# A decoder layer on one core: the shared expert's gate and up in one PSUM bank each, and smaller edits around the router

## The chip, the core and the metric

The kernel runs on one core of one Trainium2 chip. The metric is the device time of one execution in microseconds (us). TensorE multiplies matrices into PSUM; VectorE (DVE), ScalarE (ACT) and GpSimd (POOL) work on SBUF, the first two on PSUM as well; SyncE (SP) issues most of the transfers. Each engine runs its own instructions in program order and waits for the others by semaphores.

## The reference: one pre-norm decoder layer with a mixture of experts

Input are 64 blocks of 128 tokens with 128 features, and a context of 77 rows for each block. In float32:

```
x = x + SelfAttn(layernorm(x))          # 16 heads of 8, rotary, causal
x = x + CrossAttn(layernorm(x), ctx)    # 16 heads of 8, 77 keys
n = layernorm(x)
probs = softmax(n @ router_w)           # 8 experts, the last one empty
e, p = argmax(probs), max(probs)        # one expert for each token
routed = down_e( up_e(n) * silu(gate_e(n)) )       # 0 where e is the eighth
shared = down_s( up_s(n) * silu(gate_s(n)) )       # hidden size 512
x = x + 2 * p * routed + shared
```

## The kernel before

The first stage is a software pipeline over the 64 blocks. On every engine, step i does pieces of several blocks: `at(i, p, lag, piece)` runs a piece for block i - lag, so one step holds one piece of each kind, of up to nine blocks. The order of the pieces inside a step is written out by hand for each engine, and it is this order that queues the work; no planner runs at build time. The first and the last steps are unrolled, the rest is a hardware loop over pairs of steps. The second stage sorts the tokens by expert (a routing table on VectorE, rows scattered to a buffer `xs` in HBM during the first stage) and runs 70 tiles of 128 tokens through their experts; the change doesn't touch its instructions.

PSUM has eight banks of 512 float32 columns. In the first stage:

- `scores` is four banks, used as two pairs. Pair 0 takes, in turn, half of the self-attention scores for the maximum (`self_max`), half of those for the exponential (`self_exp`), the same for the cross-attention, and the shared expert: gate in its first bank, up in its second.
- `pj` takes the projections of q, k, v and of the context, and two transposes.
- `st` takes float16 transposes: the stacked q and k (`stacks`, `stacks2`, L1232) and the row maxima (`nmT_of`, L1253).
- `pv` takes the attention output (`values`, L1122), 256 columns, which VectorE transposes out (`turned`, L647).
- `ro` takes output projections (`project_out`, L1131), transposes (`xT_of`, L1139), q of the cross-attention (L1150), the router, the token positions and the shared down projection (`shared_down`, L1177), each in its own columns.

A piece of TensorE that is about to overwrite a bank calls `turn(pe, b, *users)`: the first user that is in range gives the semaphore and the count for which it waits, which is the reader of the bank's last content.

The pieces around the change, in TensorE's order of one step, with the lines of the profile: `shared_gate` (L1163), `shared_up` (L1169), the cross output projection (L1131), `nmT_of` of the self-attention (the row maxima turned, L1253), `values` of the self-attention (L1122), `positions` (L1214, L1216, L1217), `cross_exp` and `cross_max` in two turns (L1033, L1025), the context transpose (L1223), `stacks` (L1232), `shared_down` (L1177). The next step goes on with the transpose of x (L1139), a second two-turn group, the self output projection (L1131), the context projection (L1228), the transpose of x1 (L1139), and the self-attention scores (L999, L1007, L1016).

The shared expert's chain through the engines: gate on TensorE, tanh on ScalarE (L877), `half_of` on VectorE (L721), `add_cross` on VectorE (L667, the cross-attention's residual), `hidden_of` on VectorE (L727, which sets `sh_hid`), then `shared_down`, then `add_shared` on VectorE (L733). `add_attention` (L660) adds the self-attention's residual, after which TensorE transposes x1.

The router on VectorE: `logits_copy` (L682), `top_of` (L687), `marks_of` (L691: logits equal to the top, times a mark, by a scalar operand of one value per partition), `mark_top_of` (L696), `hot_of` (L700: mark equal to its maximum, again by such a scalar). GpSimd meanwhile adds the rotary products (`rope_add`, L449) and their bias (`rope_bias_in`, L453). `positions` starts with an identity matmul that puts the running counts `run_base` into PSUM (L1214) and adds this block's counts to them; `run_of` (L712) copies the new counts back, and `hot_pos_of` (L707) picks each token's row. `carry` (L604) copies one column on VectorE so that a wait has an instruction of its own to sit on, ahead of the layer norms' `bn_aggr` (L625) and of the third layer norm's `bn_stats` (L619).

Of the kernel before, what the change touches and what calls it, by code (L numbers as in the profile page):

```python
# [13 lines left out]
P = 128  # L14
# [7 lines left out]
LAG = 11  # L22
LATE = 56
# [3 lines left out]
def decoder_layer(nc, x, ctx_in, sWq, sbq, sWk, sbk, sWv, sbv, sWo, sbo,  # L27
# [16 lines left out]
    assert S == P and D == P and NB % 16 == 0 and LATE % 4 == 0 and NB >= LATE + 4 and LATE + 10 >= NB and F == 4 * P and NT % 8 == 6 and ALPHA == 2.0  # L44

    with ExitStack() as stack:
# [116 lines left out]
        run_base = sb("run_base", [P, E])  # L163
# [44 lines left out]
        st16 = st[:, :].bitcast(F16)  # L208
# [37 lines left out]
        marked = sem("marked"); mark_topped = sem("mark_topped"); hot_ready = sem("hot_ready")  # L246
# [46 lines left out]
        def run(eng, step):  # L293


            first = (LAG + 3) // 2
# [5 lines left out]
            for i in range(NB, NB + LAG):  # L302
                step(i, i % 2)
# [44 lines left out]
        def _(sync):  # L348
# [24 lines left out]
            def load_x(b, p):  # L373
                if not isinstance(b, int) or b >= 2:
                    wait(sync, rot_summed, b - 1)
                    sync.dma_start(x_in[:, p, :], x[b]).then_inc(x_in_s[p], 16)
# [6 lines left out]

# [3 lines left out]
            def rows_of_max(b, p, n):  # L387

                wait(sync, nmT_ready[n], b + 1)
                for j in range(4):  # L390
                    sync.dma_start((qkT, qkT2)[n][SLOT * j + 3 * HD:SLOT * j + 3 * HD + HG, p, 0:HG * P].rearrange("p (g q) -> p g q", g=HG),
                                   nmaxT[SLOT * j:SLOT * j + HG, n, p, :].unsqueeze(1).to_broadcast([HG, HG, P])
                                   ).then_inc(max_rows[n][p], 16)
# [13 lines left out]
            run(sync, step_and_weights)  # L407
# [19 lines left out]
        def _(pool):  # L427
# [4 lines left out]
            def ln_rstd_of(b, p, n):  # L432

                wait(pool, ln_mv[n], b + 1)
                if n == 2:
                    g.tensor_tensor(neg_mean[:, :], mv[:, 2, p, 0:1], neg_one[:, :], ALU.mult)
                g.tensor_tensor(varp[:, n:n + 1], mv[:, n, p, 1:2], eps[:, :], ALU.add).then_inc(ln_var[n], 1)
                wait(pool, ln_var[n], b + 1)
                g.tensor_tensor(rstd[:, n, p:p + 1], varp[:, n:n + 1], neg_half[:, :], ALU.pow).then_inc(ln_rstd[n], 1)  # L439

            def ln3_shift_of(b, p):

# [4 lines left out]

# [9 lines left out]

# [17 lines left out]
            def scaled(b, p, n):  # L475
                wait(pool, o_recip[n], b + 1)
                g.tensor_tensor(by_head(otok[:, n, :]), ptok[:, n, :].rearrange("p (h s) -> p h s", s=SLOT // 2)[:, :, 0:HD],  # L477
                                rsum[:, n, :].unsqueeze(2).to_broadcast([P, H, HD]), ALU.mult).then_inc(o_scaled[n], 1)

            def add_out_bias(b, p, n):  # L480

                if n == 0:
                    wait(pool, x_in_s[p], 8 * b + 16 - 8 * p)
                g.tensor_tensor(resid[:, b, :], (x_in, x1)[n][:, p, :], out_bias[:, n, :], ALU.add).then_inc(xb_ready[n], 1)  # L484
# [5 lines left out]
            def scatter(b, p):  # L490
                wait(pool, scatter_going, b)
                wait(pool, put_ready, b + 1)
                wait(pool, sh_added, b + 1)
                g.tensor_tensor(carried[:, 4:5], eps[:, :], eps[:, :], ALU.add).then_inc(scatter_going, 1)
# [896 lines left out]
```

## Time and profile before

| | before |
|---|---|
| time, median of 3 runs | 1065.71 us (1065.3 to 1066.14) |
| the profiled execution, first to last instruction | 1065.7 us |
| PE / PE weight load / DVE / ACT / POOL busy | 992.5 / 818.3 / 870.9 / 737.2 / 631.4 us |
| first stage, from first to last residual of the self-attention (L660) | 55.0 to 807.2 us, 64 blocks |
| second stage, from the first tile's gate matmul | 856.95 us on |
| granted TensorE clock, mean | 0.990 |

Matmuls are pipelined, so "PE busy" says that instructions follow each other, not that the array is at its peak. A line such as L1122 stands for all the instructions that it issued; a helper's line stands for every use. An arrow `[0.23 <-DVE arena L656]` behind a row is the idle time ahead of it and what ended it.

### The profile page before, as it was taken

How to read it: one execution, taken by the hardware profiler on the slowest of the kernel's cores; microseconds unless marked ns; L12 is line 12 of the kernel's file. 1: busy time of each engine (PE TensorE's matmuls, PEld its weight loads, DVE VectorE, ACT ScalarE, POOL GpSimd, SP SyncE). 2: the span in 40 equal slices, each digit the busy share in tenths (PEclk: the TensorE clock that was granted, in tenths of full speed). 3: DMA queues.
4: the chain of work that ended last, by engine and by line, in shares of the span. 5: the costliest groups of instructions: out<-in, count | busy, mean ns of one | idle time of the engine just before them, and what ended most of it. 6: DMA issues, size and time to landing. Idle time of an engine off the chain costs nothing.

```text
span 1065.7 us, 45022 instructions
## 1 busy us (share of the span) xinstructions
PE 992.5 (93%) x16200; PEld 818.3 (77%) x16201; DVE 870.9 (82%) x2853; ACT 737.2 (69%) x1557; POOL 631.4 (59%) x1488
## 2 busy tenths in 40 slices
PE   1579999999999999999999999999999999999995
PEld 1357777777777777777777777777777889999995
DVE  4367999999999999999999999999986457777774
ACT  0267878888888878888888888887875145555552
POOL 0346677777777677777777777767764124444443
PEclk9999999999999999999999999999999899999998
DMA  6222011000100010000100010000000122222220
GB/s 133 71 72 77 28 32 32 26 30 26 32 26 30 25 29 28 26 30 26 32 26 30 26 29 28 30 25 28 28 29 21 58 70 70 73 71 68 70 65 5
DMA packets 66648, 44.27 MB, mean 42 GB/s; under 512 B 24135, under 2 KB 61451, under 8 KB 66592
## 3 DMA queue, kind: packets, MB, share of 16 engines
q1 hardware_dynamic: 55424, 30.35, 10.5%
q0 software_dynamic: 5312, 12.18, 3.3%
q10 hardware_dynamic: 5856, 0.99, 0.7%
q8 instruction: 36, 0.59, 0.2%
q14 instruction: 20, 0.16, 0.0%
HBM read 23.96 MB, written 18.29 MB: 40 GB/s over the span
## 4 chain that ended last, share of the span: by engine, by line
PE 76%; DVE 10%; issue 4%; SPq 3%; DMA 2%; ACT 1%; POOL 1%; ACTq 1%; DVEq 0%; POOLq 0%
PE pv L1122 11%; PE scores L1302 6%; PE scores L1307 6%; PE ro L1318 6%; PE ro L1177 6%; PE scores L1163 5%; PE st L1232 5%; DVE arena L641 4%; PE scores L999 4%; PE scores L1169 4%; PE ro L1139 3%; PE pj L1145 3%; PE ro L1131 3%; PE ro L1150 2%; PE scores L1033 2%
## 5 line engine op out<-in xcount | busy, mean ns | idle before, releaser
L919 ACT ACTIVATE arena<-scores 128x1024 f32<-128x1024 f32 (+1 forms) x256 | 262.6, 1026 | 48.5 <-PE scores L1016 33.6
L641 DVE TENSOR_REDUCE arena<-scores 128x8 f16<-128x1024 f32 (+1 forms) x256 | 256.7, 1003 | 47.5 <-PE scores L1007 37.6
L859 ACT ACTIVATE arena<-st 128x128 f16<-128x128 f16 (+2 forms) x256 | 154.9, 605 | 7.9 <-PE st L1232 6.8
L859 ACT ACTIVATE arena<-arena 128x512 f16<-128x512 f32 (+2 forms) x192 | 92.9, 484 | 70.3 <-POOL arena L453 50.3
L1122 PE MATMUL pv<-arena 128*32 128x128 f32 (+1 forms) x4096 | 139.3, 277 | 0.0
L1122 PEld LDWEIGHTS pv<-arena 128*32 128x32 f32 (+1 forms) x4096 | 104.6, 110 | 17.1 <-issue 10.1
L439 POOL TENSOR_TENSOR arena<-arena,neg_half 128x1 f32<-128x1 f32 x192 | 106.5, 555 | 15.0
L449 POOL TENSOR_TENSOR arena<-arena 128x256 f32<-128x256 f32 x64 | 46.4, 725 | 78.9 <-DVE arena L633 78.9
L526 POOL DMA_INDIRECT out_dram<-x_tile x70 | 69.9, 998 | 38.5 <-POOL carried L525 26.1
L477 POOL TENSOR_TENSOR arena<-arena 128x128 f32<-128x128 f32 x128 | 51.7, 404 | 61.2 <-DVE arena L651 61.2
L1232 PE MATMUL st<-id,arena 128*128 128x128 f16 (+1 forms) x1024 | 74.0, 215 | 8.5 <-POOL arena L462 8.5
L814 DVE SCALAR_TENSOR_TENSOR half_hid<-tanh_s,scores 128x512 f32<-128x512 f32 x70 | 48.1, 688 | 40.3 <-ACT tanh_s L964 40.2
L495 POOL DMA_INDIRECT xs<-pay,put x64 | 69.5, 1085 | 13.0 <-issue 13.0
L1302 PE MATMUL scores<-xT_tile,gate_tile 128*128 128x128 f32 x560 | 75.1, 278 | 1.9 <-ACT gate_tile L859 1.6
L1318 PE MATMUL ro<-w_down,hidT 128*128 x560 | 74.1, 275 | 0.9 <-DVE x_tile L826 0.9
L1307 PE MATMUL scores<-xT_tile,up_tile 128*128 128x128 f32 x560 | 74.5, 276 | 0.0
L1163 PE MATMUL scores<-arena,ws_gate 128*128 128x128 f32 x512 | 74.3, 288 | 0.0
L1177 PE MATMUL ro<-ws_down,hidT 128*128 128x128 f32 x512 | 71.2, 282 | 2.1 <-DVE hot_pos L707 1.9
L1232 PEld LDWEIGHTS st<-id,arena 128*128 128x128 f16 (+1 forms) x1024 | 63.4, 101 | 12.0 <-POOL arena L462 10.4
L484 POOL TENSOR_TENSOR resid<-arena,out_bias 128x128 f32 (+1 forms) x128 | 58.2, 454 | 23.4 <-DVE out_bias L600 23.4
L1302 PEld LDWEIGHTS scores<-xT_tile,gate_tile 128*128 128x128 f32 x560 | 69.0, 194 | 2.3 <-issue 1.7
L1318 PEld LDWEIGHTS ro<-w_down,hidT 128*128 128x128 f32 x560 | 68.0, 192 | 1.1 <-issue 1.1
(175 smaller groups left out, 2681.3 us busy)
## 6 DMA issues: line engine op xcount, KB each, us to landing
x_tile<-xs SPq DMA_DIRECT2D x70, 129.0 KB, 2.0
arena<-arena SPq DMA_DIRECT2D x512, 4.0 KB
arena<-in_x_dram SPq DMA_DIRECT2D x64, 64.0 KB, 1.8
out_dram<-pay SPq DMA_DIRECT2D x64, 64.0 KB, 1.6
arena<-in_ctx_dram SPq DMA_DIRECT2D x64, 38.5 KB
w_gate<-in_L_ffn_gate_w_dram SPq DMA_DIRECT2D x7, 256.0 KB, 2.8
w_up<-in_L_ffn_up_w_dram SPq DMA_DIRECT2D x7, 256.0 KB, 3.1
w_down<-in_L_ffn_down_w_dram SPq DMA_DIRECT2D x7, 256.0 KB, 4.0
```

Source lines behind the costliest of these rows:

```text
L439: g.tensor_tensor(rstd[:, n, p:p + 1], varp[:, n:n + 1], neg_half[:, :], ALU.pow).then_inc(ln_rstd[n], 1)
L526: g.indirect_dma_start(out=out_rows, out_offset=bass.IndirectOffsetOnAxis(ap=x_token[:, q, :], axis=0), in_=x_tile[:, q, D:2 * D], in_offs ...
L641: v.tensor_reduce(nmax[:, n, :].rearrange("p (m r s) -> p r m s", r=2, s=SLOT)[:, u, :, 0:HG], pair(s)[:, :, 0:HG * keys].rearrange("p m ( ...
L859: return a.activation(to, of, ACT.Copy)
L919: a.activation(e32[0:rows, 2 * n + u, :], scores[0:rows, 1024 * s:1024 * (s + 1)], ACT.Exp).then_inc(sexp_done[n][u], 1)
L1122: last = t.matmul(pv[SLOT * j:SLOT * (j + 1), 0:2 * P].rearrange("p (c a y) -> p a c y", a=2, y=SLOT)[:, a], vals[0:rows, p, at0:at0 + SLO ...
L1163: last = t.matmul(scores[:, 1024 * s + c * P:1024 * s + (c + 1) * P], ws_gate[:, c * P:(c + 1) * P], xnT3[:, p, :], start=True, stop=True)
L1177: last = t.matmul(ro[:, P:2 * P], hidT[:, 0, c * P:(c + 1) * P], ws_down[:, c, :], start=c == 0, stop=c == FC - 1)
L1232: last = t.transpose(st16[:, to + g * step:to + g * step + rows], src[0:rows, g * P:(g + 1) * P], id16[0:rows, 0:rows])
L1302: last = t.matmul(sc[q][:, c * P:(c + 1) * P], gate_tile[:, q, c * P:(c + 1) * P], xT_tile[:, q, :], start=True, stop=True)
L1307: last = t.matmul(sc[2 + q][:, c * P:(c + 1) * P], up_tile[:, q, c * P:(c + 1) * P], xT_tile[:, q, :], start=True, stop=True)
L1318: last = t.matmul(ro[:, 0:D], hidT[:, p, c * P:(c + 1) * P], w_down[:, e, c, :], start=c == 0, stop=c == FC - 1)
```

## The change

- Gate goes to `pv` (all 512 columns) and up to `st` (all 512), no longer to `scores`. So `shared_gate` waits for the reader of `pv`, `shared_up` for the copy out of `st` (`qkT2_ready`, ScalarE), `self_max_turned` (the old `nmT_of` of the self-attention) for `sh_hid`, `self_values` for tanh and half, and the users of pair 0 of `scores` no longer for `sh_hid`.
- Every piece that uses `ro` or `pj` begins at column 0.
- The identity matmul in `positions` is gone. `run_of` on VectorE adds the counts of the block before (`run_pos`, two buffers) to both halves of what `positions` left, and `hot_pos_of` waits for it and reads SBUF.
- `marks_of` becomes two operations (`same_of`, `marks_of`), and they and `hot_of` are tensor_tensor operations on operands broadcast along the free dimension.
- Of the four `carry` copies per block one is left; the other waits stand alone, ahead of an earlier instruction of VectorE.
- Lags are counted from zero for each engine, and each engine is unrolled for its own lag. The order of the pieces on each engine is as before. The weight loads on SP hang on the step number (`i == 3` and `4 <= i`), so they come three steps later against SP's other pieces. Of the filler matmuls at the end of the first stage, those of three steps go. `LATE` is 60 instead of 56: the last 4 blocks, not the last 8, use four buffers of `pay`.
- Two other waits go or change: `scatter` no longer waits for `put_ready`; `project_qkv` and `ctxT_of` also wait for the readers on VectorE.

The core of the diff:

```diff
-LAG = 11
-LATE = 56
+LATE = 60
...
             def step(i, p):
-                at(i, p, 3, load_x)
-                at(i, p, 6, rows_of_max, 0)
-                at(i, p, 8, rows_of_max, 1)
-                at(i, p, 11, base_out)
-                at(i, p, 5, load_ctx)
+                at(i, p, 0, load_x)
+                at(i, p, 3, self_rows_of_max)
+                at(i, p, 5, cross_rows_of_max)
+                at(i, p, 8, base_out)
+                at(i, p, 2, load_ctx)
...
+            def same_of(b, p):
+                wait(dve, top_ready, b + 1)
+                v.tensor_tensor(same[:, :], logits[:, p, :], top[:, p:p + 1].to_broadcast([P, E]), ALU.is_equal).then_inc(same_ready, 1)
+
             def marks_of(b, p):
-                wait(dve, top_ready, b + 1)
-                v.scalar_tensor_tensor(out=mark[:, :], in0=logits[:, p, :], scalar=top[:, p:p + 1], in1=marks,
-                                       op0=ALU.is_equal, op1=ALU.mult).then_inc(marked, 1)
+                wait(dve, same_ready, b + 1)
+                v.tensor_tensor(mark[:, :], same[:, :], marks, ALU.mult).then_inc(marked, 1)
...
-                v.tensor_scalar(hot16[:, p, :], mark[:, :], mark_top[:, :], None, ALU.is_equal).then_inc(hot_ready, 1)
+                v.tensor_tensor(hot16[:, p, :], mark[:, :], mark_top[:, :].to_broadcast([P, E]), ALU.is_equal).then_inc(hot_ready, 1)
...
             def run_of(b, p):
                 wait(dve, pos_psum, b + 1)
-                v.tensor_copy(run_base[:, :], ro[:, 2 * P + E:2 * P + 2 * E]).then_inc(run_ready, 1)
+                v.tensor_tensor(run_pos[:, p, :].rearrange("p (n e) -> p n e", n=2), run_pos[:, 1 - p, E:2 * E].unsqueeze(1).to_broadcast([P, 2, E]),
+                                ro[:, 0:2 * E].rearrange("p (n e) -> p n e", n=2), ALU.add).then_inc(run_ready, 1)
...
-                v.scalar_tensor_tensor(out=half_hid[:, 0, :], in0=tanh_s[:, 0, :], scalar=1.0, in1=scores[:, 1024 * s:1024 * s + F],
+                v.scalar_tensor_tensor(out=half_hid[:, 0, :], in0=tanh_s[:, 0, :], scalar=1.0, in1=pv[:, 0:F],
...
-                v.tensor_tensor(hidT[:, 0, :], half_hid[:, 0, :], scores[:, 1024 * s + 512:1024 * s + 512 + F],
-                                ALU.mult).then_inc(sh_hid, 1)
+                v.tensor_tensor(hidT[:, 0, :], half_hid[:, 0, :], st[:, 0:F], ALU.mult).then_inc(sh_hid, 1)
...
+            ce1_turns = (((smax_done[0][0], 4),), ((sexp_done[0][0], 3),), ((smax_done[1][1], 1),), ((sexp_done[1][1], 0),),)
...
+            nm0_turns = (((sh_hid, -4),), ((qkT2_ready, -1),), ((nmT_ready[1], -2),), ((qkT_ready, 1),), ((nmT_ready[0], 0),),)
+            def self_max_turned(b, p):
+                turn(pe, b, *nm0_turns)
+                wait(pe, smax_done[0][0], b + 1)
+                t.transpose(st16[:, 0:P], nmax[:, 0, :], id16[:, :]).then_inc(nmT_psum[0], 1)
...
+            gate_turns = (((o_turned[1], 2),), ((o_turned[0], 4),), ((sh_tanh, 0), (sh_half, 0),),)
...
+                    last = t.matmul(pv[:, c * P:(c + 1) * P], ws_gate[:, c * P:(c + 1) * P], xnT3[:, p, :], start=True, stop=True)
...
+            up_turns = (((qkT2_ready, 4),), ((nmT_ready[1], 3),), ((qkT_ready, 6),), ((nmT_ready[0], 5),), ((sh_hid, 0),),)
...
-                t.matmul(cols, id32[:, :], run_base[:, :].unsqueeze(1).to_broadcast([P, 2, E]), start=True, stop=False,
-                         skip_group_check=True)
```

## Rows read from the trace of the kernel before

**Rows 1.** The page, part 1: busy time, share of the span, instructions.

```profile
PE 992.5 (93%) x16200; PEld 818.3 (77%) x16201; DVE 870.9 (82%) x2853; ACT 737.2 (69%) x1557; POOL 631.4 (59%) x1488
```

**Rows 2.** Waits from 300 to 600 us: total, times, longest, in us.

```profile
PEld ro L1139 <- DVE arena L660: 13.2, 25, 0.6
...
PEld ro L1131 <- DVE arena L656: 5.8, 25, 0.2
```

**Rows 3.** The source view of L660: count, ns min/median/max, first and last start.

```profile
L660 DVE TENSOR_TENSOR arena<-resid,ro x64: 276/279/290, 55.0 to 807.2; 128x128 f32<-128x128 f32 x64
```

**Rows 4.** Timeline of one step: start and length in us, engine, line, operation, count.

```profile
407.51 1.16 PE L1163 MATMUL scores<-arena,ws_gate 128*128 128x128 f32 x8
407.69 0.88 ACT L859 ACTIVATE arena<-st 128x824 f16<-128x824 f16 x1
...
408.40 0.97 PEld L1169 LDWEIGHTS scores<-arena,ws_up 128*128 128x128 f32 x8
...
408.71 0.60 ACT L877 ACTIVATE tanh_s<-scores 128x512 f32<-128x512 f32 x1
...
409.26 0.29 DVE L656 STREAM_TRANSPOSE arena<-arena 128x128 f32<-128x128 f32 x1
...
409.60 0.30 PEld L1131 LDWEIGHTS ro<-wc_o,arena 128*128 128x128 f32 x2 [0.23 <-DVE arena L656]
...
409.82 0.10 PEld L1253 LDWEIGHTS st<-id,arena 128*128 128x128 f16 x1
...
409.94 0.65 DVE L721 SCALAR_TENSOR_TENSOR half_hid<-tanh_s,scores 128x512 f32<-128x512 f32 x1
...
410.08 1.08 PE L1122 MATMUL pv<-arena 128*32 128x128 f32 x32
...
410.71 0.68 DVE L727 TENSOR_TENSOR hidT<-half_hid,scores 128x512 f32<-128x512 f32 x1
...
411.09 0.30 PEld L1214 LDWEIGHTS ro<-run_base,id 128*128 128x128 f32 x2 [0.20 <-issue]
...
411.23 0.18 PEld L1216 LDWEIGHTS ro<-hot,earlier 128*128 128x128 f16 x1
...
411.52 0.12 PEld L1033 LDWEIGHTS scores<-arena 28*77 28x77 f16 x2
...
412.45 1.11 PE L1177 MATMUL ro<-ws_down,hidT 128*128 128x128 f32 x8
...
413.69 0.29 DVE L733 TENSOR_TENSOR pay<-resid,ro 128x128 f32<-128x128 f32 x1 [0.30 <-PE ro L1177]
...
414.74 0.28 DVE L660 TENSOR_TENSOR arena<-resid,ro 128x128 f32<-128x128 f32 x1
...
415.07 0.33 PE L1139 MATMUL ro<-id,arena 128*128 128x128 f32 x1
```

**Rows 5.** The source view of L691, of all 64 blocks.

```profile
L691 DVE SCALAR_TENSOR_TENSOR mark<-logits,top,consts x64: 226/525/532, 97.3 to 839.7; 128x8 f32<-128x8 f32 x64
```

**Rows 6.** Timeline of the same step: router on DVE, rotary sums on POOL.

```profile
408.32 0.72 POOL L449 TENSOR_TENSOR arena<-arena 128x256 f32<-128x256 f32 x1 [1.05 <-DVE arena L633]
...
408.55 0.52 DVE L691 SCALAR_TENSOR_TENSOR mark<-logits,top,consts 128x8 f32<-128x8 f32 x1
...
409.12 0.73 POOL L453 TENSOR_TENSOR arena<-arena,rope_bias 128x256 f32<-128x256 f32 x1
...
409.48 0.39 DVE L700 TENSOR_SCALAR hot<-mark,mark_top 128x8 f16<-128x8 f32 x1
```

**Rows 7.** The source view of L604, all `carry` copies.

```profile
L604 DVE COPY carried<-eps x256: 86/139/155, 24.0 to 835.6; 128x1 f32<-128x1 f32 x128
```

**Rows 8.** Timeline of PE near 80 us: the idle time ahead of a row.

```profile
80.06 0.23 PE L1007 MATMUL scores<-arena 24*128 24x128 f16 x2 [1.12 <-DMA arena<-arena]
```

**Rows 9.** Stretch of 1 us: busy of PE, PEld, DVE, ACT, POOL, clock, DMA, GB/s.

```profile
82.00:83.00 1.00, 1.00 (x34) 0.80 (x33) 0.48 (x3) 0.61 (x3) 0.51 (x2) 0.50 0.07 16
```

**Rows 10.** Timeline of DVE in the setup.

```profile
20.62 0.15 DVE L590 CAST empty<-consts 128x1 uint32<-128x1 f32 x1 [3.44 <-DMA wc_kv<-in_L_xattn_Wv_dram]
```

More of the change, by code:

```diff
@@ L1110, in two_turns, with stack4 @@
                         round2(s2, u2, p2, g)
-            def values(b, p, n, *users):
-                vals, rows = ((val, P), (val2, C))[n]
-                wait(pe, sexp_done[n][0], b + 1)
-                wait(pe, sexp_done[n][1], b + 1)
-                turn(pe, b, *users)
+            def stack4(bank, to, src, rows, step):
+                for g in range(HG):
+                    last = t.transpose(bank[:, to + g * step:to + g * step + rows], src[0:rows, g * P:(g + 1) * P],
+                                       id16[0:rows, 0:rows])
+                return last
@@ L1158, in shared_gate, with project_cross_out @@
-            def shared_gate(b, p, s, *users):
+                last.then_inc(pv_done[0], 1)
+            pr1_turns = (((logits_ready, 0),), ((xT_ready[2], 0),), ((q2_ready, 3),), ((xT_ready[1], 3),), ((resid_done[0], 3),), ((sh_added, -1),), ((run_ready, -1),), ((resid_done[1], 0),),)
+            def project_cross_out(b, p):
+                turn(pe, b, *pr1_turns)
+                wait(pe, oT_ready[1], b + 1)
+                t.matmul(ro[:, 0:P], oT[:, 1, :], wc_o[:, :], start=True, stop=True).then_inc(proj_psum[1], 1)
@@ L1168, in shared_up @@
+            def shared_up(b, p):
+                if isinstance(b, int) and b == 0:
+                    pe.wait_ge(w_half, 1)
+                turn(pe, b, *up_turns)
                 for c in range(FC):
-                    last = t.matmul(scores[:, 1024 * s + 512 + c * P:1024 * s + 512 + (c + 1) * P], ws_up[:, c * P:(c + 1) * P], xnT3[:, p, :],
-                                    start=True, stop=True)
+                    last = t.matmul(st[:, c * P:(c + 1) * P], ws_up[:, c * P:(c + 1) * P], xnT3[:, p, :], start=True, stop=True)
@@ L1187, in busy_scores, with early, late, busy_gate @@
+            def early(i, lag, piece):
+                if isinstance(i, int) and 3 <= i < lag:
+                    piece(i - lag)
+            def late(i, lag, piece):
+                if isinstance(i, int) and NB <= i - lag and i <= NB + 7:
+                    piece(i - lag)
+            def busy_gate(b):
+                turn(pe, b, *gate_turns)
                 for c in range(FC):
-                    t.matmul(scores[:, 1024 * s + c * P:1024 * s + (c + 1) * P], w_qkv[:, 0:P], w_qkv[:, 0:P], start=True, stop=True)
@@ L1200, in busy_pj, with over @@
-            def busy_pj(b, *users):
+                    t.matmul(ro[:, 0:D], w_qkv[:, 0:P], w_qkv[:, 0:P], start=c == 0, stop=c == FC - 1)
+            def over(b, users):
                 if all(b + user[0][1] > NB for user in users):
@@ L1220, in ctxT_of @@
-            def ctxT_of(b, p, *users):
-                turn(pe, b, *users)
-                wait(pe, ctx_in_s[p], 8 * b + 16 - 8 * p)
-                t.transpose(pj[:, 3 * D:3 * D + C], ctx_t[0:C, p, :], id32[0:C, 0:C]).then_inc(ctxT_psum, 1)
-            def project_kv2(b, p, *users):
-                turn(pe, b, *users)
-                wait(pe, ctxT_ready, b + 1)
-                t.matmul(pj[0:C, 0:2 * D], ctxT[:, 0:C], wc_kv[:, :], start=True, stop=True).then_inc(kv2_psum, 1)
-            def stack4(to, src, rows, step):
-                for g in range(HG):
-                    last = t.transpose(st16[:, to + g * step:to + g * step + rows], src[0:rows, g * P:(g + 1) * P],
-                                       id16[0:rows, 0:rows])
-                return last
```

663 lines of the change are left out of this document (378 added, 285 removed).

## The prediction

> **What bounds the kernel now.** I read the page first [rows 1]: no engine but TensorE is above 90%, and VectorE follows with 82%, so either could set the pace. The waits [rows 2] show both in one loop: in each step TensorE stands once for the cross-attention's turned output (L656) and once for the residual of the self-attention (L660), both of VectorE, and no wait there is long. The steps are alike: the 64 instances of L660 lie between 55.0 and 807.2 us, so one step is (807.2 - 55.0) / 63 = 11.94 us [rows 3]. That is 752 of the 1065.7 us; what the change does is done 64 times there.
>
> The timeline of one step [rows 4] gives the loop. VectorE ends L656 at 409.26 + 0.29 = 409.55; the cross output projection starts on TensorE at 409.60. From there TensorE goes without a stop of more than 0.2 us through the turned maxima (409.82), the values (410.08), the positions (411.09), the two-turn group (411.52) and `shared_down` (412.45). VectorE waits 0.30 us for `shared_down`, adds it (413.69), reduces one set of maxima and adds the self-attention (L660, 414.74); TensorE, which waited, transposes x1 at 415.07 and makes the scores whose maxima VectorE reduces next; from there VectorE runs without a stop through the rotary products and the router back to L656. So between 409.60 and 413.69 TensorE's order is the path, and a wait that is put into that piece lengthens every step by its full length.
>
> One more thing is to be seen: the shared expert's chain runs beside this path. `hidden_of` starts at 410.71 and ends at 411.39 [rows 4]; the only one on TensorE that cares so far is the two-turn group at 411.52, since it overwrites the gate and up columns. It finds `sh_hid` 0.13 us old: a near tie.
>
> **The change part by part.**
>
> *Gate and up in `pv` and `st`.* The two-turn group at 411.52 no longer waits for `sh_hid`. But `st` is now read by `hidden_of`, and the next one to write `st` in TensorE's order is the turned maxima: `nm0_turns` begins with `(sh_hid, -4)`. In step i that piece works on block i - 2, so it waits for count i - 6; the gate of the same step works on block i - 7, whose `hidden_of` brings the count to i - 6. It is the same step's. So the wait moves forward in TensorE's order, from 411.52 to 409.82, past three pieces that don't need it. It can be over only when the chain gate, tanh, half, hidden is: if VectorE gets there as before, at 411.39, plus 0.05 us to TensorE (as from 409.55 to 409.60), so at 411.44: 411.44 - 409.82 = +1.62 us a step. Behind it stand the values, the positions and all the rest, `shared_down` included; VectorE, which comes to the values' transpose right after `hidden_of`, has nothing to do until they are there, 1.1 us later. POOL's, ScalarE's and SP's pieces that hang on the turned maxima get later by as much as their users do.
>
> `shared_up` waits for the copy of `st` by ScalarE, 407.69 + 0.88 = 408.57, and starts at 408.62 instead of 408.40. That ends its 0.97 us of loads at 409.59, just ahead of the cross projection at 409.60: it costs nothing as long as the stall behind it is there. Gate finds `pv` empty long before.
>
> *The identity matmul.* From L1214 to L1216 it is 411.23 - 411.09 = 0.14 us on the path: -0.14. The addition on VectorE replaces a copy, and `hot_pos_of` waits for it; VectorE is idle there now, and the trace has no such addition. I take 0, between 0 and one small operation, 0.14 us [rows 7]; it isn't on the path up to `shared_down`.
>
> *Carrier copies.* Three of four go, 0.139 us each [rows 7], 0.42 us a step. Those behind `hidden_of` fall into time in which VectorE now waits for the values. Only the one ahead of `half_of` is on the chain, at most 0.14.
>
> *Marks by broadcasts.* `marks_of` took 0.525 us in the median and 0.226 us at its shortest [rows 5]. In the loop it ends at 409.07, 0.03 us after POOL's rotary sum (408.32 + 0.72 = 409.04); `hot_of` ends at 409.87, 0.02 us after POOL's next (409.12 + 0.73 = 409.85) [rows 6]. So both stand until POOL is through. `same_of` starts where `marks_of` did and reads logits and another small SBUF tensor, so I let it stand until 409.07 too; the new `marks_of` then meets POOL's next sum at 409.12, and `hot_of` still ends with that one. If `marks_of` gets in first, `half_of` starts as before, give or take the copy: I take 0. If not, it stands until 409.85, and the four small pieces between it and `half_of` follow: 409.94 becomes some 410.44, +0.5. If none of the three stands, two operations of 0.23 replace 0.53, `hot_of` loses 0.2 and a copy goes: -0.3, which tanh (ended 409.31) still allows.
>
> The Trainium skill, page "SBUF — State Buffer", section "SBUF: two separate sides", has a rule for this: GpSimd and a VectorE operation with two SBUF inputs exclude each other for a whole instruction, whoever starts first. The trace agrees, 0.525 against 0.226 us for an operation with two such inputs. By that rule all three new operations are held, and the broadcasts win nothing: it is the case of +0 or +0.5, not of -0.3.
>
> *Clock.* After TensorE had stood 1.12 us ahead of 80.06 [rows 8], the granted clock was 0.50, the 1.2 GHz level, around 82 us [rows 9]. The new stall is longer: from the end of the cross projection's loads (409.90) to 411.44, 1.5 us. A spell at half clock that falls on `shared_down` adds about its 1.11 us. How many of the steps get one the trace can't say, since it has few such gaps; between none and 30 I take 12: +13 us.
>
> *Ends.* The shared weights are no longer loaded in the setup, where VectorE stands 3.44 us for the last of the small weights [rows 10]: between 0 and -3.4, I take -2. The expert weights lie three steps later in SP's queue, ahead of the rows of maxima; those have more time now, 0. Fewer fillers may leave the first expert tile at half clock: at most one gate's 0.97 us, +1. The four-buffer mode, the shorter unrolling and the dropped `put_ready`: 0, since no row of the loop waits there.
>
> **The sum.** Gate and maxima meet in steps 7 to 65, 59 of them. 59 x (1.62 - 0.14) = 87; -2 + 1 + 13 for the rest. The profiled execution took 1065.7 us, and the median of the runs is the same: 1065.7 + 99 = 1165 us.
>
> **The rivals.**
>
> - *VectorE is what counts (faster).* Its step gets shorter by 0.42 for the copies and 0.07 + 0.2 for the router, 0.7 us, 64 times: 1065.7 - 44 = 1022. For it: 82% busy, and it is in the loop. Its place is the arrival of `sh_hid` at TensorE: it decides once that is there at 409.82, 1.6 us earlier than now. Against it: tanh alone ends at 409.31, and half and hidden take 1.45 us from start to end [rows 4]. 4%.
> - *The copies of the wait don't bite*, because another user comes first and the order stays as it was: within 0.2%, which is about what a measurement of this kernel can tell from no change. 2%.
> - *The small operations don't stand for POOL*: the stall is 0.3 shorter, 59 x 1.18 = 70, and less clock is lost, 7: 1065.7 + 70 - 1 + 7 = 1142. 13%.
> - *`marks_of` loses against POOL's second sum*: 59 x 0.5 = 30 more: 1195. This is what the skill's rule gives if POOL starts first. 13%.
> - *The clock falls in most steps*, 45 x 1.11 = 50 instead of 13: 1202. For it: a shorter gap was enough once. Against it: some of the matmuls around the stall are float32 at full size, and in the loop before it never fell. 10%.
>
> **How the numbers follow.** The forecast has 58%; its own range is 1150 to 1180. With the cases at 1142 and 1195 whole, and part of the one at 1202, the range is 1128 to 1208. Faster 0.04, same 0.02, slower 0.94 are the sums of the cases.
>
> **What would show it.** In the trace after: idle time ahead of the self-attention's turned maxima, ended by `hidden_of`, some 1.5 us in each step (no such wait: the whole is wrong); a wait of VectorE for the values behind `hidden_of`; steps of 13.4 us between residuals; `same_of` of 0.5 us where POOL adds, and `marks_of` of 0.16 (of 0.7: POOL came first); the clock row with digits under 9 in the first stage (none: 13 us less); first blocks starting 2 us earlier. If the step is 11.9 us or shorter, the path was not what I took it for.

## The result, and the profile after

| | before | after |
|---|---|---|
| time, median of 4 runs | 1065.93 us (1065.30 to 1068.59) | 1153.94 us (1152.61 to 1159.47) |
| span of the profiled execution | 1065.7 us | 1152.5 us |
| residual additions of the self-attention, first to last | 55.0 to 807.2 us | 52.2 to 897.0 us |
| step in the loop | 11.95 us | 13.39 us |

The changed kernel is slower: its time is 1.0849 times that of before (95% interval 1.0825 to 1.0874). In the changed kernel the lines have other numbers: the self-attention's residual is L717, its turned maxima L1233, its values L1244, gate L1297, up L1306, the cross projection L1254, half L780, hidden L786.

The page of the changed kernel, parts 1 and 2, against [rows 1]:

```profile
PE 998.0 (87%) x16024; PEld 812.3 (70%) x16025; DVE 874.0 (76%) x2725; ACT 744.4 (65%) x1557; POOL 633.2 (55%) x1488
...
PEclk9999999999999999999999999999999989999998
```

Every engine has the busy time of before within 1%, and the span is 87 us longer: hardly any work was added, all engines stand more. (VectorE has 128 instructions fewer and 3 us more to do.) The clock row in tenths is too coarse for what is said of the clock below.

The waits of the changed kernel between 300 and 600 us (total, times, longest), against [rows 2]:

```profile
...
DVE arena L679 <- PE pv L1244: 30.8, 22, 1.4
PEld st L1233 <- DVE hidT L786: 28.1, 22, 1.3
ACT arena L923 <- PE st L1233: 26.8, 22, 1.2
PE st L1233 <- DVE hidT L786: 23.9, 22, 1.1
...
PEld ro L1189 <- DVE arena L717: 12.5, 22, 0.6
```

The first four are new, each once in a step: TensorE stands 1.3 us at the turned maxima until `hidden_of` is through (1.1 us counted by its matmuls, the PE row, instead of its weight loads, the PEld row), VectorE stands 1.4 us for the values behind it, ScalarE 1.2 us for the maxima. They are one stall, seen from three engines.

The timeline of one step of the changed kernel, to be laid beside [rows 4]:

```profile
425.19 0.28 DVE L717 TENSOR_TENSOR arena<-resid,ro 128x128 f32<-128x128 f32 x1
...
430.87 0.52 DVE L746 TENSOR_TENSOR same<-logits,top 128x8 f32<-128x8 f32 x1
...
431.13 0.97 PEld L1306 LDWEIGHTS st<-arena,ws_up 128*128 128x128 f32 x8 [0.18 <-ACT arena L923]
...
431.18 0.60 ACT L944 ACTIVATE tanh_s<-pv 128x512 f32<-128x512 f32 x1
431.43 0.17 DVE L750 TENSOR_TENSOR mark<-same,consts 128x8 f32<-128x8 f32 x1
431.45 0.74 POOL L467 TENSOR_TENSOR arena<-arena,rope_bias 128x256 f32<-128x256 f32 x1
...
431.81 0.30 DVE L713 STREAM_TRANSPOSE arena<-arena 128x128 f32<-128x128 f32 x1
...
432.23 0.30 PEld L1254 LDWEIGHTS ro<-wc_o,arena 128*128 128x128 f32 x2
432.23 0.65 DVE L780 SCALAR_TENSOR_TENSOR half_hid<-tanh_s,pv 128x512 f32<-128x512 f32 x1
...
433.07 0.68 DVE L786 TENSOR_TENSOR hidT<-half_hid,st 128x512 f32<-128x512 f32 x1
...
433.80 0.10 PEld L1233 LDWEIGHTS st<-id,arena 128*128 128x128 f16 x1 [1.28 <-DVE hidT L786]
...
433.96 1.08 PE L1244 MATMUL pv<-arena 128*32 128x128 f32 x32
...
435.11 0.37 ACT L952 ACTIVATE arena<-pj,arena 128x128 f32<-128x128 f32 x1 [0.77 <-PE pv L1244]
435.11 0.45 DVE L679 STREAM_TRANSPOSE arena<-pv 128x256 f32<-128x256 f32 x1 [1.36 <-PE pv L1244]
...
435.71 0.14 PEld L1201 LDWEIGHTS pj<-id,arena 77*128 77x128 f32 x1 [0.34 <-issue]
435.72 0.28 PE L1201 MATMUL pj<-id,arena 77*128 77x77 f32 x1 [0.19 <-ACT arena L952]
...
436.30 1.11 PE L1313 MATMUL ro<-ws_down,hidT 128*128 128x128 f32 x8
```

Counted from the residual addition ahead of it, `hidden_of` ends where it ended before: 433.75 - 425.19 = 8.56 us, against 411.39 less the start of the addition one step of 11.97 us earlier (414.74 - 11.97 = 402.77), 8.62. What has moved is TensorE: its turned maxima stood at 409.82 - 402.77 = 7.05 in the step and now stand at 433.80 - 425.19 = 8.61, behind `hidden_of` instead of ahead of it. From there on the two steps have nearly the same lengths: maxima to context transpose 2.05 before (409.82 to 411.87 in the trace of before), 1.91 after; `shared_down` to the next residual addition 2.29 before, 2.30 after (it is at 438.60).

The source views of the changed kernel (count, ns min/median/max, first and last start), against [rows 3, 5]:

```profile
L717 DVE TENSOR_TENSOR arena<-resid,ro x64: 275/278/289, 52.2 to 897.0; 128x128 f32<-128x128 f32 x64
L746 DVE TENSOR_TENSOR same<-logits,top x64: 166/524/528, 93.0 to 927.0; 128x8 f32<-128x8 f32 x64
L750 DVE TENSOR_TENSOR mark<-same,consts x64: 166/167/168, 93.5 to 927.2; 128x8 f32<-128x8 f32 x64
```

The addition to the time sits between the first and the last residual: 844.9 us instead of 752.2, +92.7. Ahead of the first one the changed kernel is 2.9 us shorter, behind the last one 3.0 us; 92.7 - 5.9 = 86.8, which is the difference of the spans. All but 9 of the 92.7 are steps of 13.39 us. Those 9 come from six steps of 14.9 us, evenly spaced (they end between 303 and 712 us), in each of which the clock is granted at its lower level for a while. One of these stretches (PE, PEld, DVE, ACT, POOL busy, clock, DMA, GB/s):

```profile
299.00:302.40 3.40, 3.40 (x34) 2.96 (x32) 1.47 (x7) 2.05 (x4) 2.64 (x9) 0.53 0.02 4
```

Clock 0.5 is the lower level, 1.2 GHz; the row covers hardly more than the stretch. It begins some 2 us behind a stall like all the others (the maxima at 296.77, after 1.09 us of standing by the PE row), and it falls on `shared_down`, which starts 2.5 us behind the maxima in the step above.

### The profile page after: what moved, and what is told of

Read it like the earlier page. It is cut to its first block, busy times and chain, and to the rows that moved or that the text cites. A ratio compares the mean times of both kernels' runs of the same rounds, so it can differ in the third digit from the quotient of the medians.

```text
span 1152.5 us, 44908 instructions
## 1 busy us (share of the span) xinstructions
PE 998.0 (87%) x16024; PEld 812.3 (70%) x16025; DVE 874.0 (76%) x2725; ACT 744.4 (65%) x1557; POOL 633.2 (55%) x1488
## 4 chain that ended last, share of the span: by engine, by line
PE 35%; DVE 22%; issue 19%; POOL 17%; SPq 2%; DMA 1%; ACTq 1%; ACT 1%; POOLq 1%; DVEq 0%
PE scores L1414 6%; PE scores L1419 5%; PE ro L1430 5%; PE pv L1244 3%; PE ro L1313 3%; POOL xs L513 3%; DVE arena L667 3%; DVE arena L659 2%; DVE arena L661 2%; DVE hidT L786 2%; POOL arena L463 2%; POOL arena L467 2%; DVE arena L698 2%; POOL arena L454 2%; POOL arena L447 2%
## 5 line engine op out<-in xcount | busy, mean ns | idle before, releaser
L490 POOL TENSOR_TENSOR arena<-arena 128x128 f32<-128x128 f32 x64 | 25.9, 405 | 151.9 <-DVE arena L683 151.9
L673 DVE TENSOR_REDUCE arena<-scores 128x8 f16<-128x1024 f32 x64 | 78.4, 1225 | 26.4 <-PE scores L1092 26.4
L679 DVE STREAM_TRANSPOSE arena<-pv 128x256 f32<-128x256 f32 x64 | 28.8, 450 | 88.4 <-PE pv L1244 88.4
L463 POOL TENSOR_TENSOR arena<-arena 128x256 f32<-128x256 f32 x64 | 46.4, 725 | 69.3 <-DVE arena L661 69.3
L985 ACT ACTIVATE arena<-scores 128x1024 f32<-128x1024 f32 x64 | 65.5, 1024 | 27.0 <-PE scores L1101 27.0
L667 DVE TENSOR_REDUCE arena<-scores 128x8 f16<-128x1024 f32 x64 | 76.5, 1195 | 3.2 <-PE scores L1092 2.2
L1313 PE MATMUL ro<-ws_down,hidT 128*128 128x128 f32 x512 | 76.8, 297 | 2.4 <-DVE run_pos L766 2.3
L1306 PE MATMUL st<-arena,ws_up 128*128 128x128 f32 x512 | 73.8, 287 | 0.5 <-ACT arena L923 0.2
L1297 PE MATMUL pv<-arena,ws_gate 128*128 128x128 f32 x512 | 72.4, 284 | 0.0
L1233 PE MATMUL st<-id,arena 128*128 128x128 f16 x64 | 14.8, 231 | 64.5 <-DVE hidT L786 63.9
L1306 PEld LDWEIGHTS st<-arena,ws_up 128*128 128x128 f32 x512 | 62.0, 191 | 11.6 <-ACT arena L923 11.3
L1244 PE MATMUL pv<-arena 128*32 128x128 f32 x2048 | 70.0, 278 | 0.1
```

What stands on the lines that cost most here:

```text
L667: v.tensor_reduce(nmax[:, 0, :].rearrange("p (m r s) -> p r m s", r=2, s=SLOT)[:, 0, :, 0:HG], pair(0)[:, :, 0:HG * P].rearrange("p m (g k ...
L673: v.tensor_reduce(nmax[:, 0, :].rearrange("p (m r s) -> p r m s", r=2, s=SLOT)[:, 1, :, 0:HG], pair(1)[:, :, 0:HG * P].rearrange("p m (g k ...
L1244: last = t.matmul(pv[SLOT * j:SLOT * (j + 1), 0:2 * P].rearrange("p (c a y) -> p a c y", a=2, y=SLOT)[:, a], val[0:P, p, at0:at0 + SLOT], ...
L1297: last = t.matmul(pv[:, c * P:(c + 1) * P], ws_gate[:, c * P:(c + 1) * P], xnT3[:, p, :], start=True, stop=True)
L1306: last = t.matmul(st[:, c * P:(c + 1) * P], ws_up[:, c * P:(c + 1) * P], xnT3[:, p, :], start=True, stop=True)
L1313: last = t.matmul(ro[:, 0:D], hidT[:, 0, c * P:(c + 1) * P], ws_down[:, c, :], start=c == 0, stop=c == FC - 1)
```

## The experiments

Two theories were open once the trace was read. The first: the place of one wait on TensorE makes the loss, whatever bank the projections lie in. The second: the change of banks, or the small edits on VectorE, cost something by themselves, and the wait is only where it shows.

### The wait alone, in the kernel before

```diff
-                at(i, p, 3, nmT_of, 0, ((qkT2_ready, -1),), ((nmT_ready[1], -2),), ((qkT_ready, 1),), ((nmT_ready[0], 0),))
+                at(i, p, 3, nmT_of, 0, ((sh_hid, -4),), ((qkT2_ready, -1),), ((nmT_ready[1], -2),), ((qkT_ready, 1),), ((nmT_ready[0], 0),))
```

> The kernel before, with one wait added and nothing else: the turned maxima of the self-attention wait for sh_hid of the same step. Theory: +1.62 us in 59 steps, and some 6 spells of half clock of 1.5 us: 1065.7 + 96 + 9 = 1170 us, step 13.56 us. Rival (a wait there is hidden, since VectorE and not TensorE sets the pace): 1066 us.

One run took 1163.25 us, the median of before on that chip 1065.47. The step is 13.49 us. Its waits between 300 and 600 us:

```profile
...
DVE arena L647 <- PE pv L1122: 31.7, 22, 1.4
PE st L1253 <- DVE hidT L727: 31.7, 22, 1.4
```

And its source view of the residual addition:

```profile
L660 DVE TENSOR_TENSOR arena<-resid,ro x64: 276/277/289, 54.6 to 905.8; 128x128 f32<-128x128 f32 x64
```

This kernel has no other banks and none of the small edits, and it loses at least as much as the change: VectorE stands as long for the values (31.7 us in 22 waits against 30.8), and TensorE stands at the same place, there 0.35 us longer (31.7 against 23.9, PE rows). The one wait is enough.

### One projection back at a time, then both

Gate back in `scores`, up left in `st` (the waits go with it):

```diff
-                    last = t.matmul(pv[:, c * P:(c + 1) * P], ws_gate[:, c * P:(c + 1) * P], xnT3[:, p, :], start=True, stop=True)
+                    last = t.matmul(scores[:, c * P:(c + 1) * P], ws_gate[:, c * P:(c + 1) * P], xnT3[:, p, :], start=True, stop=True)
...
-            V0_turns = (((sh_tanh, -3), (sh_half, -3),), ((o_turned[1], -2),), ((o_turned[0], 0),),)
+            V0_turns = (((o_turned[1], -2),), ((o_turned[0], 0),),)
```

> The changed kernel, but gate is again in the first bank of pair 0 of scores (up stays in st). Theory: the turned maxima still wait for sh_hid, and the chain to it is the same; step 13.4 us, 1152 us within 5. Rival (gate in pv, which the values wait for, costs its own part): faster by 20 us or more.

Up back in `scores`, gate left in `pv`:

```diff
-                    last = t.matmul(st[:, c * P:(c + 1) * P], ws_up[:, c * P:(c + 1) * P], xnT3[:, p, :], start=True, stop=True)
+                    last = t.matmul(scores[:, 512 + c * P:512 + (c + 1) * P], ws_up[:, c * P:(c + 1) * P], xnT3[:, p, :], start=True, stop=True)
...
-            nm0_turns = (((sh_hid, -4),), ((qkT2_ready, -1),), ((nmT_ready[1], -2),), ((qkT_ready, 1),), ((nmT_ready[0], 0),),)
+            nm0_turns = (((qkT2_ready, -1),), ((nmT_ready[1], -2),), ((qkT_ready, 1),), ((nmT_ready[0], 0),),)
```

> The changed kernel, but up is again in the second bank of pair 0 of scores (gate stays in pv). Theory (the step is longer by the wait for sh_hid ahead of the turned maxima): that wait is gone, and what is left is the wait of the self-attention's values for half_of, which ends about 0.56 us after the values could start: step 11.94 + 0.56 - 0.14 = 12.36 us, about 1085 us in all. Rival (the added operations on VectorE and the shared first columns make it slow): nothing of that is undone, so about 1150 us.

Both back, that is both diffs together, all the small edits of the change kept:

> The changed kernel, but gate and up are both again in pair 0 of scores; the counts, marks, copies, lags and weight loads stay as changed. Theory: no stall; the identity matmul saves 0.14 us a step, while the two-part marks put the cross-attention's second transpose 0.23 us later, which is now on the path: step 12.03 us, 59 x 0.09 = 5 more, 6 less at both ends: 1065 us, no change. Rival (the small edits are a gain of their own): step 11.8 us, about 1051 us.

Measured on one chip (before 1065.47): gate back 1159.73 us (one run), step 13.39; up back 1094.57 us (one run), step 12.39; both back 1077.30 (4 runs, 1074.92 to 1083.32), ratio 1.0116 (1.0073 to 1.016), step 12.13. The source view of the residual addition, gate back:

```profile
L717 DVE TENSOR_TENSOR arena<-resid,ro x64: 276/279/290, 53.5 to 902.1; 128x128 f32<-128x128 f32 x64
```

Up back:

```profile
L717 DVE TENSOR_TENSOR arena<-resid,ro x64: 276/279/290, 52.2 to 832.5; 128x128 f32<-128x128 f32 x64
```

Both back:

```profile
L717 DVE TENSOR_TENSOR arena<-resid,ro x64: 276/278/290, 52.3 to 819.6; 128x128 f32<-128x128 f32 x64
```

Up in `st` makes the wait: with up taken back, the step is 1.00 us shorter with gate in `pv` (13.39 to 12.39) and 1.26 with gate in `scores` (13.39 to 12.13). Gate taken back alone gives nothing: the step is the 13.39 that was expected. Its time lies 7.7 us above the expected 1152, outside the "within 5": in this execution eight steps of the loop, not six, have a stretch at the lower clock, with stalls of the same length (28.1 us in 22 waits of L1233 from 300 to 600 us, as in the changed kernel).

With up out of the way, gate in `pv` costs 0.26 us by itself (12.39 against 12.13): in that kernel VectorE waits up to 0.4 us for the values in each step, which may not overwrite `pv` until half is through. The two prices don't add up, since the values stand behind the maxima in TensorE's order: who has waited for hidden finds half done.

The step with up back, 12.39 against the expected 12.36, was hit partly by chance: gate in `pv` had been given 0.56 us and costs 0.26, and the small edits, of which only the identity matmul had been counted, cost 0.18. The time missed its 1085 by 9.6 us: about half lies behind the last residual (260.2 us, 255.5 in the changed kernel), and one early step takes 15.0 us.

The last kernel missed both numbers given for it (1065 and 1051). The small edits are no gain: the step is 0.18 us longer than before and three steps early in the loop take 13.7, 13.2 and 16.1 us. The timeline of TensorE in these steps:

```profile
102.14 0.23 PE L1092 MATMUL scores<-arena 24*128 24x128 f16 x2 [1.61 <-DMA arena<-arena]
...
115.31 0.23 PE L1092 MATMUL scores<-arena 24*128 24x128 f16 x2 [1.06 <-DMA arena<-arena]
...
128.86 0.29 PE L1092 MATMUL scores<-arena 24*128 24x128 f16 x2 [1.42 <-DMA arena<-arena]
```

The scores wait for their rows of maxima, which SP issues behind the three loads of an expert's weights; from 129 to 135 us the granted clock is 0.50, its lower level. In the changed kernel the longest such wait between 80 and 130 us is 0.33 us: the longer step hid it.

Where the 0.18 us come in, a step of the loop shows:

```profile
433.76 0.29 DVE L717 TENSOR_TENSOR arena<-resid,ro 128x128 f32<-128x128 f32 x1
...
440.37 0.30 DVE L713 STREAM_TRANSPOSE arena<-arena 128x128 f32<-128x128 f32 x1
...
440.79 0.30 PEld L1254 LDWEIGHTS ro<-wc_o,arena 128*128 128x128 f32 x2 [0.48 <-issue]
440.82 0.46 PE L1254 MATMUL ro<-wc_o,arena 128*128 128x128 f32 x2 [0.32 <-DVE arena L713]
```

VectorE's transpose of the cross-attention ends 440.67 - 433.76 = 6.91 us into the step, against 409.55 - 402.77 = 6.78 before, and TensorE waits for it ahead of the cross projection. The two-part marks stand ahead of that transpose. With the marks in one operation (the next kernel told of) the step falls to 11.99 us.

### The marks, and where the loads lie

From the kernel with both projections back, step by step: marks as one operation on SBUF; the same reading the logits from PSUM; and that with the shared weights' load at step 0 and the experts' at steps 1 to 7.

```diff
-                v.tensor_tensor(mark[:, :], same[:, :], marks, ALU.mult).then_inc(marked, 1)
+                v.scalar_tensor_tensor(out=mark[:, :], in0=logits[:, p, :], scalar=top[:, p:p + 1], in1=marks,
+                                       op0=ALU.is_equal, op1=ALU.mult).then_inc(marked, 1)
...
-                v.scalar_tensor_tensor(out=mark[:, :], in0=logits[:, p, :], scalar=top[:, p:p + 1], in1=marks,
+                v.scalar_tensor_tensor(out=mark[:, :], in0=ro[:, 0:E], scalar=top[:, p:p + 1], in1=marks,
...
-                if isinstance(i, int) and i == 3:
+                if isinstance(i, int) and i == 0:
```

> Gate and up both in scores, and marks_of is again one scalar_tensor_tensor with a scalar operand; the rest as changed. Theory (the second small operation, not the scalar operand, puts the cross-attention's second transpose 0.23 us later, and that is on the path here): the step goes from 12.13 to about 11.9 us, 59 x 0.23 = 13 us less than with two parts: 1062 us. Rival (broadcasts are cheaper than scalar operands): slower than with two parts.

> As the one before, but marks_of reads the logits from PSUM (ro, where the router left them) instead of their copy in SBUF; it still has the scalar operand and the marks in SBUF. Theory (it stands for GpSimd because it has two tensor inputs in SBUF): it takes 0.23 us instead of 0.53 in the loop, the transpose behind it comes up to 0.3 us earlier, until shared_up's end on TensorE is the limit: step 11.7 us, about 1050 us. Rival (the scalar operand is what stands for GpSimd): still 0.53 us, step 11.9 us, 1062 us.

> As the one before, but the shared weights are loaded at SP's step 0, behind the wait for the setup's small weights, and the experts' at steps 1 to 7 (three steps earlier than in the changed kernel, as in the kernel before). Theory (late weight loads stand in SP's queue ahead of the rows of maxima and cost two or three steps 1 to 4 us each, which the long step of the changed kernel hid): about 6 us less, 1044 us, with the start as early as in the changed kernel. Rival (the long early steps come from half clock alone): no change.

Measured on one chip, 10 runs each beside a median of before of 1063.96: 1071.11, ratio 1.0057 (1.0034 to 1.0079); 1069.35, ratio 1.0036 (1.0015 to 1.0057); 1063.48, ratio 0.9976 (0.9956 to 0.9997). The steps are 11.99, 11.94 and 11.95 us in the mean.

The marks missed: 1062 us with a step of 11.9, and 1050 with 11.7, had been expected. One operation instead of two is worth 0.14 us a step, not 0.23, and reading PSUM some 0.05 more, not 0.2. The rival to the first (broadcasts are the cheaper form) is out, and so is the rival to the second (the marks would still take 0.53 us).

Moving the loads took 5.9 us off the median, about the 6 that the theory on them gave; the 1044 that went with it stood on the 1050 of the kernel ahead of it. The profiles show a part of it only: their spans are 1065.2 and 1062.8 us, and of TensorE's waits for the rows of maxima above 0.4 us, between 80 and 170 us, the first has four (0.45 to 1.21 us), the second two (0.74 and 1.07 us).

What became of the second kernel's marks, by the source views of both kernels (the operand in SBUF, then in PSUM) and the timeline of one of the second's steps:

```profile
L750 DVE SCALAR_TENSOR_TENSOR mark<-logits,top,consts x64: 226/525/532, 93.4 to 848.8; 128x8 f32<-128x8 f32 x64
L750 DVE SCALAR_TENSOR_TENSOR mark<-ro,top,consts x64: 225/226/228, 93.5 to 838.8; 128x8 f32<-128x8 f32 x64
```

```profile
506.33 0.60 ACT L944 ACTIVATE tanh_s<-scores 128x512 f32<-128x512 f32 x1
506.64 0.73 POOL L467 TENSOR_TENSOR arena<-arena,rope_bias 128x256 f32<-128x256 f32 x1
506.69 0.70 DVE L759 TENSOR_TENSOR hot<-mark,mark_top 128x8 f16<-128x8 f32 x1
507.41 0.65 DVE L781 SCALAR_TENSOR_TENSOR half_hid<-tanh_s,scores 128x512 f32<-128x512 f32 x1
```

The marks never stand for POOL any more, 0.226 us in the median instead of 0.525. But the hot marks now begin 0.05 us behind POOL's second addition instead of near its end, and end 0.02 us behind it. Half starts behind them, 0.48 us after the tanh. The hold has moved to the next operation with two SBUF inputs, and little is won: TensorE comes earlier to the cross scores in `scores`, and stands there for `hidden_of` (waits from 300 to 600 us; the kernel ahead of it has no such row):

```profile
PE scores L1118 <- DVE hidT L787: 8.8, 22, 0.4
```

The same marks in the changed kernel:

> The changed kernel (gate in pv, up in st), but marks_of is one operation that reads the logits from PSUM. Theory (the router's small operations on VectorE stand ahead of half_of and so of sh_hid, on the path): half_of starts 0.4 us earlier, at the end of tanh; step 13.0 us, 23 us less: 1130 us. Rival (gate and tanh alone set sh_hid): step 13.39 us, 1153 us.

One run: 1158.66 us, step 13.30 instead of the expected 13.0. The hot marks, median 0.18 us in the changed kernel, here:

```profile
L759 DVE TENSOR_TENSOR hot<-mark,mark_top x64: 124/699/707, 95.2 to 931.3; 128x8 f16<-128x8 f32 x64
```

The time isn't better although the step is 0.09 us shorter, because in this execution eleven steps of the loop, not six, have a stretch at the lower clock, about 1.5 us each.

### The order on VectorE ahead of hidden

If the wait for `hidden_of` is what costs, each tenth of a microsecond that VectorE spends between the tanh and the end of `hidden_of` is a tenth of the step. So the hot marks and the cross residual were put behind `hidden_of` (diff against the kernel just told of; the wait ahead of LN1's variance stands one instruction earlier):

```diff
-                at(i, p, 7, hot_of)
                 at(i, p, 0, ln1_mean_var)
                 at(i, p, 7, half_of)
-                at(i, p, 6, add_cross)
                 at(i, p, 7, hidden_of)
+                at(i, p, 6, add_cross)
+                at(i, p, 7, hot_of)
```

> The changed kernel with the one-operation marks that read PSUM, and on VectorE the cross residual add and the hot marks moved from ahead of half and hidden to behind them (LN1's variance stands where it stood, its wait one instruction earlier). Theory (the price of the change is the stretch from the tanh to the hidden layer, which the identity matmul now waits for; what VectorE does in it counts one for one): half starts at the tanh's end instead of 0.44 us behind it, hidden follows at once, so it ends 0.45 to 0.5 us earlier: step 12.85, time 1130 to 1135. Rival (other work of the step, such as the rope chain or the positions behind the hot marks, is late next): step 13.2 to 13.3, time 1153 to 1159. Rival (the end comes from TensorE's own work, not from the wait): unchanged at 13.3.

One run took 1114.63 us (before on that chip: 1065.42), the step 12.80. The timeline of a step:

```profile
427.80 0.60 ACT L944 ACTIVATE tanh_s<-pv 128x512 f32<-128x512 f32 x1
...
428.43 0.69 DVE L781 SCALAR_TENSOR_TENSOR half_hid<-tanh_s,pv 128x512 f32<-128x512 f32 x1
...
429.15 0.69 DVE L787 TENSOR_TENSOR hidT<-half_hid,st 128x512 f32<-128x512 f32 x1
...
429.89 0.10 PEld L1233 LDWEIGHTS st<-id,arena 128*128 128x128 f16 x1 [0.95 <-DVE hidT L787]
...
429.95 0.16 DVE L759 TENSOR_TENSOR hot<-mark,mark_top 128x8 f16<-128x8 f32 x1
```

From the tanh's end to the end of `hidden_of` it is now 1.44 us; it was 1.97 in the changed kernel (431.78 to 433.75). The step answers about one for one: 0.53 us less there, 0.59 less in the step (0.50 less than in the kernel just told of). The 15 us by which the time undercuts the expectation go with the clock: no step of the loop behind 65 us has a stretch at the lower level in this execution. Against the kernel just told of, 59 steps of 0.50 us and eleven stretches of about 1.5 us make 46 us, an estimate; the spans differ by 44 (1156.8 and 1112.8). That the shorter stall of TensorE (0.95 us instead of 1.28 in the changed kernel) is what spares the clock is not shown by itself.

The last kernel takes the same thought to the best one so far (both projections back, marks from PSUM, loads moved): there the hot marks go behind the cross residual, ahead of `hidden_of`, and again the wait ahead of LN1's variance stands one instruction earlier.

> The kernel with both projections back in the scores' bank, marks in one operation from PSUM and the shared weights loaded a step apart from the experts, and the hot marks moved on VectorE from ahead of half to behind the cross residual add, so that GpSimd's rope addition no longer holds half through them. Theory: half starts 0.45 us earlier, but the positions (which wait for the hot marks) and the cross scores (which wait for hidden) gain only some 0.15 us: step 11.8, time 1055, ratio 0.99. Rival (the positions become the late ones, or the hot marks are held by GpSimd's next addition): step 11.96 or more, ratio 0.998 to 1.005.

6 runs, median 1057.63 us (1055.01 to 1060.83), ratio to before 0.9933 (0.9915 to 0.9951): 0.7% below the kernel before, a small difference but clear of noise, and it has neither gate nor up in the new banks. That is nearer to the theory (0.99) than to the rival (0.998 or more). Its steps alternate between 11.66 and 12.07 us, 11.87 in the mean (theory 11.8), and none of them has a stretch at the lower clock; two early steps take 12.4 and 12.5 us, which took 13.8 and 15.6 in the kernel that it was made from:

```profile
L717 DVE TENSOR_TENSOR arena<-resid,ro x64: 275/279/290, 53.3 to 799.1; 128x128 f32<-128x128 f32 x64
```

## Why the prediction was right

**The path and the wait.** "It is the same step's" is the sentence that decides the case, and it held: the first user in `nm0_turns` is the hidden layer made in the same step, and the kernel with nothing but that wait shows the whole loss (1163.25 us). The forecast for the wait and the identity matmul together was 1.62 - 0.14 = 1.48 us a step, 87 us in all. Measured against the step of [rows 4] it is 13.39 - 11.97 = 1.42, and what of the 92.7 us isn't the clock is 92.7 - 9.3 = 83.4 us.

**The terms inside it.** The turned maxima moved by 8.61 - 7.05 = 1.56 us, not 1.62; the 0.06 is `hidden_of` ending that much earlier in the step. The identity matmul's 0.14 is there as 2.05 - 1.91 from the maxima to the context transpose, so that 1.56 - 0.14 is the 1.42 measured. But it isn't won where it was taken out: from the values to the context transpose it is 1.79 before and 1.75 after, since that transpose now waits for an operation of ScalarE (L952) that stands for the values. The other 0.10 lies between the maxima and the values (0.26 before, 0.16 after), whose operands had time to get ready.

**A price that the stall hides.** The cross projection starts 7.04 us into the step instead of 6.83. The prediction looked for such a delay in the later `shared_up` and gave it nothing, "as long as the stall behind it is there". The amount is right, since the maxima wait for VectorE anyway, but the cause is another: VectorE's transpose ahead of the projection ends at 6.92 instead of 6.78, behind the two-part marks. With both projections back `shared_up` isn't late any more, and the projection still starts 7.03 us into the step (440.79 - 433.76); with the marks in one operation that reads PSUM, and up left in `st`, it starts 6.80 us into it (432.95 - 426.15). The prediction asked of the marks only what they do to `half_of`.

**Marks.** "`same_of` of 0.5 us where POOL adds, and `marks_of` of 0.16": 0.524 and 0.167 in the median, the latter never above 0.168. The taken case (`marks_of` gets in ahead of POOL's second addition) was the right one, by 0.02 us: in this step `marks_of` starts at 431.43 and POOL's addition at 431.45. The Trainium skill's rule on the page "SBUF — State Buffer", section "SBUF: two separate sides" (such an operation and GpSimd's exclude each other for a whole instruction, whoever starts first) is borne out by the pair of runs that differ in one operand: 0.525 us with both inputs in SBUF, 0.226 with one of them in PSUM. That is one direction; that GpSimd's operation would stand in its turn is not seen here, where L467 takes 0.741 us in the median behind marks that got in first, and 0.727 in the kernel whose marks end ahead of it (both projections back, one operation on SBUF). What the prediction didn't draw from it: an operation freed from the hold may only bring the next one into it, as the hot marks were.

**Clock.** That some steps get a stretch at the lower level was right. The size, 13 us against 9.3, was near by luck: 12 steps at 1.11 us were taken, and it was six at 1.55, half the number at a higher price. The rival with the clock falling in most steps is out for this kernel. Why six steps and not others fall, with the same stall in all of them, is open; the count was eight with gate back, where the stall is the same, eleven in the kernel whose stall is 0.17 us longer in the mean (1.45 against 1.28), and none at 0.95 us. The kernel with the wait alone, whose stall is longer still, has only four such steps, three of them of 15.7 us. So the length of the stall alone doesn't set the count.

**Ends.** Predicted -1, measured -5.9. The start was 2.9 us shorter, where -2 was taken. The 3.44 us stand for the last of the small weights [rows 10] is 0.34 us in the changed kernel:

```profile
17.64 0.15 DVE L608 CAST empty<-consts 128x1 uint32<-128x1 f32 x1 [0.34 <-DMA wc_kv<-in_L_xattn_Wv_dram]
```

The 3.0 us at the other end weren't foreseen, and they hardly come from the change. From the last residual to the first tile's gate matmul it is 49.7 us before and 46.4 after. The execution of before that was profiled had a stretch at the lower clock there (granted 0.57 from 825 to 833 us). The kernel with the wait alone, which ends the stage as before does, takes 46.8 us without such a stretch. At the first tile, where the predicted +1 was looked for, both kernels have one, that of the changed kernel longer (0.57 from 940 to 948 us, against 0.63 from 857 to 861); from that matmul to the end it takes 209.1 us instead of 208.75, so the +1 was 0.3.

**Expert weights at 0** was right for this kernel alone. Its steps are long enough for the rows of maxima behind the loads. With a step of about 12 us the move of the loads brought 5.9 us in the median.

The miss of 11 us (1165 against 1154) is then 3.6 from the wait (87 against 83.4), 3.7 from the clock, 4.9 from the ends, together 12.2, less some 1.2: the median of the changed kernel's runs lies 1.4 us above the span of its profiled execution, where before the two lay 0.2 us apart. The prediction took the span and the median of before as equal, and that was chance: where both are known for one execution, the time is 1.8 us above the span (1154.33 and 1152.5 for the changed kernel), so the profiled execution of before was some 1.6 us longer than the median one.

## What to carry to other kernels

When a tile moves to another bank, look up who writes that bank next in the engine's order, and at which count its wait is over: a wait on the same step's result ties two chains that ran side by side, and its price is about the difference of their positions in the step, which the timeline of the kernel before already shows (1.62 us by it, 1.56 measured). Once such a wait stands, each operation that another engine has ahead of the awaited one is on the path, so the order of that engine has to be changed with the banks. An edit that costs nothing beside a stall is to be priced again when the stall goes.

## What was not expected of the hardware

- A hold between GpSimd and VectorE moves on: marks from 0.525 to 0.226 us, hot marks from 0.18 to 0.70 us, and the step of the changed kernel only 0.09 us shorter for it.
- Stalls of TensorE of nearly the same length and 13.4 us apart led to the lower clock level in 6 of some 60 steps in one kernel and in 8 in another (stalls of 1.28 us in both), in 11 with 1.45 us, and in none behind 65 us with 0.95 us, each in one profiled execution. From the third to the last the step lost 0.50 us, and the eleven stretches of about 1.5 us went as well.
